# The end of a gated delta-rule stage as a stream of tiles, with the next layer's norm and logits inside it

## What is computed

```python
# delta-rule attention, H = 4 heads, 64 keys and 128 values per head
o = gated_delta_rule(q, k, v, g, beta)
o = rmsnorm(o, o_norm_w) * silu(gate)
x = x + o.reshape(b, t, 512) @ Wo            # x1
h2 = layernorm(x, ln2_g, ln2_b)
x_out = gelu(h2 @ W2 + b2) + x
# outer residual, then the expert layer on layernorm(x)
logits = xn @ Wr + br
idx = argmax(logits); gate = softmax(logits)[idx]
y = gelu(xn @ W1[idx] + b1[idx]) @ W2[idx] + b2[idx]     # 8 experts, 256 -> 1024 -> 256
out = x + y * gate
```

## Time and profile before

| | before |
|---|---|
| median of 3 runs | 848.73 us (847.96 to 853.16) |
| the profiled execution | 848.96 us |
| its span, first to last instruction | 847.3 us |
| mean granted TensorE clock | 0.899 of 2.4 GHz |
| PE busy | 676.9 us (80%) |
| DVE, ACT, POOL busy | 417.6, 328.4, 136.7 us |

### The profile page before, as it was taken

How to read it: one execution, slowest core, us unless ns; L and a number is a source line. 1 busy time by engine, 2 the same in 40 slices (tenths; PEclk the granted TensorE clock), 3 DMA queues, 4 the chain that set the end, 5 groups by cost and what they waited for, 6 DMA issues and landing times. The chain is left out here.

```text
span 847.3 us, 18840 instructions
## 1 busy us (share of the span) xinstructions
PE 676.9 (80%) x7638; PEld 520.7 (61%) x7638; DVE 417.6 (49%) x903; ACT 328.4 (39%) x881; POOL 136.7 (16%) x189
## 2 busy tenths in 40 slices
PE   3778887789899999976785989989986751689980
PEld 2456665565566666654663567589985550689970
DVE  5446886765435545424676266646556452011111
ACT  1244453443544455424666152512233230234420
POOL 1011112202100000004334420370000103000003
PEclk9889999999999999996889679979998775699995
DMA  6920000002500000004000000000000037951103
GB/s 169 352 73 3 1 2 1 1 14 109 129 1 2 1 2 2 2 1 125 2 2 2 1 1 2 1 2 1 2 1 1 0 114 250 346 199 38 38 32 100
DMA packets 33865, 44.99 MB, mean 53 GB/s; under 512 B 7904, under 2 KB 28768, under 8 KB 33664
## 3 DMA queue, kind: packets, MB, share of 16 engines
q1 hardware_dynamic: 29568, 34.35, 12.5%
q0 software_dynamic: 2064, 7.74, 2.6%
q10 hardware_dynamic: 2160, 1.89, 0.7%
HBM read 36.24 MB, written 7.73 MB: 52 GB/s over the span
## 5 line engine op out<-in xcount | busy, mean ns | idle before, releaser
L392 ACT ACTIVATE a_pr<-a_bank,a_nms 128x160 f32<-128x160 f32 x128 | 49.1, 391 | 56.9 <-DVE a_nms L722 54.5
L858 PE MATMUL a_bank<-ident,a_pr 128*80 128x128 f32 x256 | 40.3, 282 | 26.4 <-DVE a_pt L698 23.2
L2084 ACT ACTIVATE f_hb<-f_bank,cols 128x128 f32<-128x128 f32 x96 | 35.2, 367 | 55.7 <-PE f_bank L2201 50.4
L858 PEld LDWEIGHTS a_bank<-ident,a_pr 128*80 128x80 f32 x256 | 25.1, 121 | 46.7 <-ACT a_pr L392 32.1
L2201 PE MATMUL f_bank<-f_xts,f_w 128*128 x384 | 50.3, 288 | 0.8 <-DVE f_xts L2154 0.8
L2201 PEld LDWEIGHTS f_bank<-f_xts,f_w 128*128 128x128 f32 x384 | 48.9, 203 | 1.7 <-issue 1.2
L628 DVE TENSOR_REDUCE a_negmx<-a_bank 128x2 f32<-128x320 f32 x64 | 30.4, 475 | 31.8 <-PE a_bank L850 31.8
L698 DVE COPY a_pt<-a_bank 80x512 f32<-80x512 f32 x60 | 41.0, 683 | 9.5 <-PE a_bank L858 8.8
L2211 PE MATMUL f_bank<-f_w,f_hb 128*128 128x256 f32 x192 | 44.0, 383 | 0.0
L2211 PEld LDWEIGHTS f_bank<-f_w,f_hb 128*128 128x128 f32 x192 | 36.1, 193 | 4.5
L357 POOL TENSOR_TENSOR a_spr<-a_linv,a_hm 128x128 f32<-128x128 f32 x32 | 12.1, 400 | 146.2 <-DVE a_linv L677 133.6
(11 more groups left out here) (359 smaller groups left out, 1539.6 us busy)
## 6 DMA issues: line engine op xcount, KB each, us to landing
f_w<-in_f_w SPq DMA_DIRECT2D x16, 1024.0 KB, 9.4
a_ct<-in_ctxt SPq DMA_DIRECT2D x15, 160.0 KB, 4.7
rows<-in_rows SPq DMA_DIRECT2D x1, 2120.0 KB, 11.1
slots_x<-a_zero POOLq DMA_DIRECT2D x1, 1920.0 KB, 7.2
slots_y<-a_zero POOLq DMA_DIRECT2D x1, 1920.0 KB, 12.6
f_xs<-slots_x ACTq DMA_DIRECT2D x13, 128.0 KB, 2.0
slots_y<-f_yb POOLq DMA_DIRECT2D x12, 128.0 KB, 2.0
x<-in_x SPq DMA_DIRECT2D x2, 512.0 KB, 5.0
```

The source lines that it names most:

```text
L392: i = act.activation(pr[:, p, j, k, :], s_bank[j][:, k * KW:(k + 1) * KW], ACT.Exp, bias=nms[:, p, j, k:k + 1], accum_out=rsum[:, p, 2 * j ...
L858: m = pe.transpose(dst[0:HK, (2 * k + a) * P:(2 * k + a + 1) * P], pr[:, p, j, k, a * HK:(a + 1) * HK], c.ident[:, :])
L2084: act.activation(hb[:, m, :], bank[m % 4][:, 0:P], ACT.Gelu, bias=c.col("f_b1", e * FC + m)).then_inc(z["act"], 1)
```

## The change

- The turn of the values moves ahead of the inversion; ACT copies them from PSUM and POOL, no longer DVE, multiplies by beta.
- The rest of stage_e becomes a loop of 10 iterations in which tile t is at `dl`, `o`, tile t-1 at `ogt`, `enc`, `x1` and its norm's statistics, and tile t-2 at `xt2` and W2. Inverse roots are Ln and Exp per tile, not one Sqrt and a reciprocal. After tiles 0 to 3 and after the last come Gelu and the last add, then the expert layer's norm (Ln and Exp over four tiles), transposes and logits, which stage_f did.
- Slots hold 514 numbers a row: normed row, x, gate, row number. stage_f scatters these (8 DMAs, one per tile, rows of 2,056 bytes where they had 1,024), POOL keeps each tile's x, gate and row numbers aside (`xk`, `row`), DVE forms `x + y * gate` on the tile, and POOL scatters the finished rows to the output. The gather, the last DVE pass and `finish` go. One buffer is cleared in the first stage, not two.

```diff
@@ stage_e, gpsimd @@
+            for t in range(NT):
+                pool.wait_ge(z["vtc"], t + 1)
+                pool.tensor_tensor(bv[:, t, :, :], bv[:, t, :, :], beta[...], ALU.mult).then_inc(z["bv"], 1)
             pool.wait_ge(z["rss"], 2)
@@ stage_e, scalar @@
             inverse_lengths(0, bank[0][:, 0:32].rearrange("p (t h) -> p t h", h=HG))
+            for t in range(NT):
+                act.wait_ge(z["vt"], t + 1)
+                act.activation(bv[:, t, :, :].rearrange("p h n -> p (h n)"), bank[t], ACT.Copy).then_inc(z["vtc"], 1)
...
-            act.activation(osd[:, :], oss[:, :], ACT.Sqrt, scale=1.0 / VD, bias=eps[:, 0:1]).then_inc(z["osd"], 1)
...
+            for t in range(NT + 2):
+                if t < NT:
+                    act.wait_ge(z["dl"], t + 1)
+                    act.activation(de[:, t, :, :]..., bank[0], ACT.Copy).then_inc(z["de"], 1)
+                if t > 1:
+                    u_ = t - 2
+                    act.wait_ge(z["xt2p"], u_ + 1)
...
+                    for k in range(KC):
+                        a = act.activation(xt2[:, u_ % 2, k, :], bank[5][:, k * P:(k + 1) * P], ACT.Identity,
+                                           scale=c.col("e_g2", k), bias=c.col("e_b2", k))
+                    a.then_inc(z["xt2"], 1)
+                if 0 < t <= NT:
+                    act.wait_ge(z["ogt"], t)
+                    act.activation(de[:, t - 1, :, :]..., bank[3], ACT.Copy).then_inc(z["ogs"], 1)
+                if t < NT:
+                    act.wait_ge(z["o"], t + 1)
+                    act.activation(bv[:, t, :, :]..., bank[1 + t % 2], ACT.Square).then_inc(z["osq"], 1)
+                    act.wait_ge(z["oss2"], t + 1)
+                    act.activation(olog[:, head], oss2[:, head], ACT.Ln, scale=1.0 / VD, bias=eps[:, 0:1]).then_inc(z["olog"], 1)
+                    act.wait_ge(z["olog"], t + 1)
+                    act.activation(orr[:, head], olog[:, head], ACT.Exp, scale=-0.5).then_inc(z["orr"], 1)
+                if 0 < t <= NT:
+                    act.wait_ge(z["mv2"], t)
+                    act.activation(lrs[:, t - 1:t], w.mv[:, t - 1, 1:2], ACT.Ln, bias=eps[:, 2:3]).then_inc(z["lrs"], 1)
+                    act.wait_ge(z["lrs"], t)
+                    act.activation(rs2[:, t - 1:t], lrs[:, t - 1:t], ACT.Exp, scale=-0.5).then_inc(z["rs2"], 1)
+                if t in (5, 9):                       # 4 Gelus (L1692 before)
...
+                if t in (6, 9):                       # Ln and Exp of the expert layer's norm
...
+                if t in (7, 9):                       # 2 copies of turned rows, xtf
...
@@ stage_e, vector @@
+            for t in range(NT + 2):
+                if t < NT:                            # reduce_sum -> oss, times rq2 -> oss2
...
+                if t > 1:                             # W2's bias -> hb (b2)
...
+                if t < NT:
+                    dve.wait_ge(z["orr"], t + 1)
+                    dve.tensor_tensor(ors[:, head], orr[:, head], rq[:, t, :], ALU.mult).then_inc(z["ors"], 1)
+                    dve.wait_ge(z["ors"], t + 1)
+                    for hh in range(HG):
+                        a = dve.scalar_tensor_tensor(bv[:, t, hh, :], bank[1 + t % 2][:, hh * VD:(hh + 1) * VD],
+                                                     ors[...], gw[:, t, hh, :], ALU.mult, ALU.mult)
+                    a.then_inc(z["og"], 1)
+                if 0 < t <= NT:                       # x1, bn_stats, bn_aggr, wait rs2, tensor_scalar -> xn2
...
@@ stage_e, tensor: in each iteration @@
+                # apply -> dl (t) | xt2p (t-2), waits xn2 | ogt (t-1), waits og | apply -> o (t), waits de
+                # W2 -> f2 (t-2), waits xt2 | Wo -> enc (t-1), waits ogs, x1 | at t = 7 and after the loop: routes()
@@ stage_f @@
-            sp.dma_start(wr[:, :, :], c.d["f_wr"]...).then_inc(z["small"], 16)
+            sp.dma_start(ids[:, :], c.d["f_ids"]).then_inc(z["ids"], 16)     # behind before, ones, tab
...
+            def write(e, i):                          # POOL, for each tile
+                pool.wait_ge(z["xs"], i * 16 + 32)
+                pool.tensor_copy(xk[:, (i + 1) % 2, :], xs[:, D:WX]).then_inc(z["kept"], 1)
...
+                pool.wait_ge(z["yb"], i + 2)
+                pool.indirect_dma_start(out, bass.IndirectOffsetOnAxis(ap=row[:, 0:1], axis=0), yb[:, :], None,
+                                        bounds_check=N - 1, oob_is_err=False).then_inc(z["stored"], 16)
+                pool.wait_ge(z["stored"], i * 16 + 16)
+                pool.sem_inc(z["rows_out"], 1)
...
             def hidden(e, i):                         # ACT, for each tile
                 act.wait_ge(z["xst"], i + 1)
+                act.wait_ge(z["kept"], i + 1)
                 act.dma_start(xs[:, :], slots[...]).then_inc(z["xs"], 16)
```

More of the change, by code:

```diff
@@ L38 @@
 MAXT = E - 1 + N // P
+WX = 2 * D + 2
 COLS, ROWS = {}, {}
@@ L82, in stage_semaphore @@
     return ctx.taken[-1]
[L86 to L139, removed]
 def stage_abc(nc, c):
@@ L1796, in _ @@
[L1796 to L1805 removed]
+            dve.wait_ge(z["gw"], NT)
@@ L1807, in _ @@
+            dve.wait_ge(z["logits"], 1)
+            dve.tensor_tensor(c.lg[:, :, :], bank[5][:, 256:320].rearrange("p (t n) -> p t n", n=E),
+                              c.row("f_br").unsqueeze(1).to_broadcast([P, NT, E]), ALU.add).then_inc(z["lg"], 1)
         @block.tensor
@@ L1903, in _ @@
             lengths(0, z["ssq"])
-            pe.wait_ge(z["gate"], NT)
-            pe.wait_ge(z["lss"], 2)
+            for t in range(NT):
+                pe.wait_ge(z["gate"], t + 1)
+                if t == 0:
+                    pe.wait_ge(z["lss"], 2)
+                for hh in range(HG):
+                    a = pe.transpose(bank[t][:, hh * P:(hh + 1) * P], qkv[:, 4 + hh, t * P:(t + 1) * P], c.ident[:, :])
+                a.then_inc(z["vt"], 1)
+            pe.wait_ge(z["vtc"], 4)
             def product(dst, lhs, rhs, g):
@@ L1937, in _, with apply @@
             pe.wait_ge(z["xt"], 8 * (LEVELS - 1) + 4)
[L1938 removed]
+            def apply(dst, mats, vec, t, done):
                 for hh in range(HG):
[L1940 to L1950 removed]
@@ L1984, in stage_f @@
+            routes(1)
+def stage_f(nc, c, out):
     with stage_semaphores(nc) as ctx:
@@ L2011, in stage_f @@
         yb = sb("yb", [P, D])
-        yg = sb("yg", [P, NT, D])
-        s = ln_sems(sem, "ln")
-        z = sems("small zero logits lg mx sh ex se rse eq cand ix hot rank tot run cmp more cnt pri first posa "
-                 "posb posh pos posi ends scattered xs xst xts hid act ypr yb stored gathered xout")
+        z = sems("small ids ncopy xcopy kept row rows_out mx sh ex se rse eq cand ix hot rank tot run cmp more cnt pri first posa "
+                 "posb posh pos posi ends scattered xs xst xts hid act ypr yb2 yb stored")
         s_w = [sem(f"w{e}") for e in range(E)]
@@ L2067, in _ @@
+                pool.wait_ge(z["stored"], i * 16 + 16)
+                pool.nop(nofuse=True)
+                pool.sem_inc(z["rows_out"], 1)
+            tiles(pool, write)
         @block.scalar
         def _(act):
-            ln_scalar(act, s, c.w)
-            xt_scalar(act, s, bank, xt)
-            act.wait_ge(z["sh"], NT)
+            for t in range(NT):
+                act.activation(xb[:, t, 0:D], c.xn[:, t, :], ACT.Copy).then_inc(z["ncopy"], 1)
+            act.wait_ge(z["sh"], 1)
@@ L2231, in build @@
         c.xn = sb("xnorm", [P, NT, D])
+        c.lg = sb("logits", [P, NT, E])
         c.ident = sb("ident", [P, P])
@@ L2262, in build @@
             stage_e(nc, c)
-        stage_f(nc, c)
-        finish(nc, c, out)
-def finish(nc, c, out):
-    with nc.semaphore("stored") as stored, nc.Block() as block:
-        @block.sync
-        def _(sp):
-            sp.dma_start(out.rearrange("(t p) d -> p t d", p=P), c.x[:, :, :]).then_inc(stored, 16)
-            sp.wait_ge(stored, 16)
+        stage_f(nc, c, out)
 def kernel(**inputs):
```

361 lines of the change are left out of this document (202 added, 159 removed).

## The result

| | before | after |
|---|---|---|
| median | 850.10 us (4 runs beside it) | 896.42 us (891.46 to 899.69, 4 runs) |
| the profiled execution, its span | 848.96, 847.3 us | 899.69, 898.0 us |
| mean granted TensorE clock | 0.899 | 0.873 of 2.4 GHz |

The changed kernel takes 1.0537 times the time of the kernel before (95% interval 1.0475 to 1.0599). The forecast was 878 us in a range of 860 to 900: the side and the mechanism of the stream held, the size was 18 us short. The profiled execution is the slowest of the four, 3.3 us above their median, so a sum over its trace comes out about 3 us larger than the medians do.

The account below looks back on a forecast made before the run. It took chains of waits to bound the kernel, with one engine working while others wait in the rewritten part. Terms 4.0 + 36.5 + 4.7 + 4.0 - 19.9 = +29.3 on 848.96 gave 878 us, range 860 to 900.

Parts of the forecast that it names:

- The alternation: In the stream, Ln and Exp each need their own table load: 38 loads, 48.8 us of ACT.
- The 1,380 ns of drain: Rival on table loads: each costs twice its row, 36 on the path give +46, 925 us; chance 0.02.
- The loop of one iteration: In the stream, from one tile's `rs2` Exp to the next: 10.15 us at PE's full clock, three of four loads whole.
- The clock: In the stream: 107.0 us at full clock, 128.6 at 1.2 GHz; middle 118 taken against 81.5, +36.5 (+25.5 to +47.1).
- a denser PE wins it back: In the stream: part of each iteration runs at the lower clock, but denser PE work regains it; hence the middle, 118.
- The turn: Values turned ahead of the inversion: PE goes on later there, +4.0 us (+3.6, up to +6).
- The head of stage_f: From stage_f's start to the scatter's end: `posi` at F+10.1, last scatter landing in 3.5, +4.7 us (+2.3 to +7).
- The tile loop: Stage_f's loop over tiles: steady part at no cost with 1.3 us of slack, start later under weights, +4 (0 to +9).
- a sign that it is wrong: In the tile loop: the forecast is wrong if the loop waits for `kept`.
- the rival of the tile loop that waits for rows: Scatter and load take over 1.3 us more, each further microsecond paid in some ten tiles; at 1 us, 888; chance 0.10.
- The end: From the last W2 product to the end: 5.0 us remain of 24.9, -19.9 (-20.5 to -18.5).
- The rival without the alternation: One set serves Ln and Exp: 34 loads go, loop 7.4 us, stream 81 or 88, total 845 (834 to 855); chance 0.06.

Follow-up runs that it names:

- one_table: Changed kernel with the table set holding both Ln and Exp chosen by hand before the stream and behind each group of Gelus: 865.39 us, 1.0143 of before.
- filler: Changed kernel with ten extra 128x128 identity products per stream iteration on PE, where it waits: 895.33 us, 1.0539 of before.
- values_ahead: Kernel before with only the turn of the values moved ahead of the inversion, with ACT's copies and POOL's products: 853.05 us, 1.0034 of before.
- weights_late: Changed kernel with expert 2's weights too started only when the first scatter is done: 897.57 us, 1.0537 of before.
- end_kept: Kernel before with only the last stage's part of the change, POOL keeping the next tile's columns before waiting for the last landing: 834.82 us, 0.9829 of before.
- end_only: Kernel before with only the last stage's part of the change (514-number rows, finished rows scattered to the output, no gather): 839.87 us, 0.9882 of before.
- end_kept_late: The end_kept kernel with the third expert's weights held back until the scatter has landed: 835.84 us, 0.9845 of before.

## Why the prediction was right in kind and short in size

- **The alternation: right.** 38 loads, 1.283 us each, one hidden and three whole in each tile. one_table took 30.1 us off the stream by two added lines. That also shows that a set with both functions exists; in these programs the builder picks it only when told to. The Trainium skill (ScalarE: Activation LUTs, Table sets: the hidden batching unit) counts one load for Ln then Exp: the set does hold both, but these traces have a load at each until the set is chosen by hand. The 1,380 ns of drain that the Trainium skill adds to each load (the same page, What ACT_TABLE_LOAD costs) are not seen: every one of the loads above is followed by its activation within 0.02 us of its end unless data is late. An estimate by that page's figure, for the 29 loads that are followed directly by their activation: the stream would have been some 40 us longer still.
- **The loop of one iteration: right.** 10.15 us at full clock was forecast; filler shows 10.3 at a granted clock of 1.00.
- **The clock: mis-sized, 6.2 us in the stream.** The sum took the middle, 118, between 107.0 at full clock and 128.6 at half. The granted clock was 0.70 over the stretch, so 0.6 of the time at half, and by the forecast's own ends that gives 107.0 + 0.6 x 21.6 = 120, and 4 us stay over. Against the parts of the forecast at full clock the 17.3 us more than 107.0 lie so: the first two `og` 17.4 us for 14.4, the next four tiles 46.8 for 40.8, the two with the blocks in their way 26.9 for 25.1, from the last `og` to the last `rs2` 16.5 for 12.7, from there to `lg` 16.7 for 14.0. So the step that was too small is "a denser PE wins it back": that holds for the middle in part (0.79), and not for the last 38.3 us, at 0.59. PE stands on the path there: 16 logits products took 3.42 us where the kernel before had 3.94 for 32. How much of the 6.5 us of the last two parts is the clock was not run by itself.
- **The turn: right in size, in part by luck** (+4.6 for +4.0). In after PE turned the values below the full clock (granted 0.70), 5.35 us, so the inversion's first product came 5.7 us behind the Ln; in values_ahead 3.69 and 4.05 us, where the forecast said 3.6 later than before's 0.4. What the turn costs there is 1.3 us net, since PE's clock does not fall ahead of the inversion (1.00 in the first 8.4 us, 0.77 in the kernel before). The forecast counted no such gain inside the inversion (2.4 us in values_ahead, 0.7 in after); in after a turn 1.7 us longer stands in its place.
- **The head of stage_f: mis-sized, 3.2 us.** `cand` at F+3.3 (F+4.3 forecast) and `posi` at F+9.1 (F+10.1) were early by 1.0. The last scatter landed in 7.64 us where 3.5 were taken and 5 was the bound. The prediction had noted that experts 0 to 2 still load and priced it from a scatter that ran behind them; weights_late shows that the third expert's traffic is the whole difference. The stretch, +7.9, lies outside the forecast's own bounds for it (+2.3 to +7).
- **The tile loop: mis-sized, 3.6 us.** The steady part was forecast at no cost with 1.3 us of slack. Its times leave 2.6 us for a load (started 2.1 us before a tile, there 0.5 behind its start). It took 2.8 us at the median and 3.65 in the late tile shown, and from `yb` to the load's start 4.5 us passed, not 4.0 (869.57 to 874.04). So the slack was just used up, and only some tiles wait: 1.8 us in nine. The loop does wait for `kept`, which the forecast had named as a sign that it is wrong; the rival of the tile loop that waits for rows was half true, its mechanism is there, at 0.2 us a tile. The start of the loop cost 5.8 us, all of the forecast's +4 and more: 1.9 by the late copy, 0.5 with the wider rows and 3.4 with the stream ahead of it, as end_kept shows.
- **The end: mis-sized, 2.4 us.** From the last W2 product to the end 7.3 us, not 5.0. The last scatter is issued 2.1 us after the product's end, nearly as forecast (0.95 + 0.9), but 5.2 us pass from there to the end of the span, where 2.5 + 0.6 were taken. By the windows of the trace the DMA engines move nothing and no engine is busy from 895.0 on, so the landing was as forecast and some 3 us stand where 0.6 were taken for the barrier and the last waits. What they are spent on the trace does not show. The -17.5 lies outside the bounds given (-20.5 to -18.5).
- **Ahead of the changed part: not forecast, 5.4 us**, about 3 of them in every kernel with the values ahead (below). The range held no term for stretches that the change does not touch.
- **The rival without the alternation** had its loop right (7.4 us, measured 7.37) and the rest too low: 81 us at full clock or 88 at 0.75, where one_table took 94.2 at 0.78. The time outside the loop, filling and draining, is what both sums had too small.

Together 0.6 + 6.2 + 3.2 + 3.6 + 2.4 + 5.4 = 21.4 us, which is the 50.7 less the 29.3 forecast. All six errors have one sign. The three largest in the changed part are one kind of error: the clock, the scatter's landing and the load of xs were priced between what the kernel before shows and a bound, and the change itself moved each of them towards the bound or past it. That the total, 896.42, still lies in the range of 860 to 900 is in part luck: two terms and the untouched stretches lie outside their bounds, and the stream, 4.4 us under its own, and the loop make up for them.

## What to carry to other kernels

Before a stage is made into a stream per tile, list ACT's functions of one tile in order and look in the trace at which pairs have a table load between them; if there are any, choose the set that holds both by hand, once outside the loop. A stream over few tiles pays for filling and draining (35 us on top of eight loops of 7.4 here), so its loop must win more than that over the steps. Work that is moved out of a stage may have been the cover of a load: with norm and logits gone from ahead of the scatter, the same scatter and the same loop took longer. Run the parts of a change alone: here the other end of it, without the stream, is 1.7% faster than the kernel before. In a loop over one buffer, whatever frees the buffer must not stand behind the landing of a store in its engine's program: moving one copy ahead of one wait gave 5.2 us of loop in end_kept and 3.7 in the changed kernel.

## What the runs showed of the hardware that was not expected

**Stretches that no edit touches were longer with the values ahead.** The Ln starts at 550.6 to 553.0 us in the four kernels that turn the values in the old place (before, end_only, end_kept, end_kept_late) and at 553.4 to 558.6 in the eight that turn them ahead. Part of this lies in two places of an early stage, where the work is the same. The windows of the kernel before and then of the kernel after at the first place, and then at the second, each from the same instruction:

```profile
165.00:170.00 5.00, 4.61 (x71) 4.05 (x72) 2.33 (x8) 2.15 (x9) 0.00 (x0) 1.00 0.00 0
```

```profile
167.05:172.05 5.00, 4.61 (x40) 3.99 (x44) 2.13 (x7) 2.15 (x9) 0.00 (x0) 0.68 0.00 0
```

```profile
208.90:218.90 10.00, 7.10 (x54) 4.37 (x55) 7.09 (x14) 4.82 (x12) 3.51 (x1) 1.00 1.05 330
```

```profile
212.60:222.60 10.00, 7.09 (x51) 4.25 (x49) 7.05 (x14) 4.82 (x12) 3.51 (x1) 0.87 1.03 278
```

PE is as busy with fewer products, at a lower granted clock. From the reduction of DVE at 164.17 to the one at 169.80 the kernel before takes 5.63 us and the kernel after 7.23; from 208.93 to 226.89 it is 17.96 and 19.60. All eight kernels with the values ahead have both steps, 1.6 us and 1.4 to 1.6, at a clock of 0.66 to 0.68 and of 0.85 to 0.87; the four others have neither, at 1.00 in both places. Why the clock is lower there, in values_ahead nearly 390 us ahead of its first changed instruction, stays open. The rest of the spread is no mark of the second kind: end_only alone starts its Ln 1.9 us later than the kernel before, and the executions of the kernel before, 847.96 to 854.28 us in all, differ by more, at granted clocks of 0.903 to 0.891. So values_ahead's 1.0034 does not price the moved turn by itself: 3.5 us of its profile's 3.6 us lie ahead of it.

**A scatter's landing depends on what else loads.** The same scatter of 128 rows of 2,056 bytes landed in 3.2 us (end_only), 3.6 (weights_late) and 7.6 (after). The DMA share was 0.42 in the first (719.0 to 722.3), 0.43 in the second (776 to 780) and 1.00 in the third (776 to 781).
